# Audio tower on one Trainium2 core: the rows of the first layer normalisation written by GpSimd and not by ScalarE

## The reference, cut to what matters

```
def _layernorm(x, axis=-1, eps=1e-05):
    m = jnp.mean(x, axis=axis, keepdims=True)
    v = jnp.var(x, axis=axis, keepdims=True)
    return (x - m) / jnp.sqrt(v + eps)
...
    h = _L0_tok_ref(x, ...)
    h = h + _L0_attn_ref(_layernorm(h, axis=-1), L0_attn_kernel)
    h = h + _L0_ffn_ref(_layernorm(h, axis=-1), L0_ffn_W1, ...)
```

## Time and profile before

| what | value |
|---|---|
| runs | 116.94, 117.05, 117.34 us; median 117.05 |
| span of the profiled execution | 114.5 us |
| total time of the profiled execution | not printed apart; 117.05 - 114.5 = 2.55 us lie around the span if it is like the median |
| busy shares of the span | PE 83%, DVE 80%, PEld 65%, ACT 59%, POOL 52% |
| mean granted TensorE clock | 0.969 of full speed, full in the middle of the kernel |

### The profile page before, as it was taken

One profiled execution on the slowest core, in us unless ns is written; L12 is line 12 of the kernel. 1 busy time (PEld: TensorE's weight loads), 2 busy tenths in 40 slices (PEclk: granted clock), 3 DMA queues, 4 the chain that ended last, 5 costly groups with the idle time before them and its releaser, 6 DMA issues.

```text
span 114.5 us, 2381 instructions
## 1 busy us (share of the span) xinstructions
PE 94.5 (83%) x618; PEld 74.7 (65%) x618; DVE 91.1 (80%) x335; ACT 67.9 (59%) x207; POOL 59.4 (52%) x122
## 2 busy tenths in 40 slices
PE   6968889899899999999999989997979827994000
PEld 2344367779588888888888979886848625773000
DVE  2789999999999799799797899996899999824000
ACT  3051447946868968968969888947587504550000
POOL 3335795754767767677586565290350996000000
PEclk9999999999999999999999999999999999999755
DMA  3940000000100100100000000000000021333332
GB/s 66 214 172 0 0 0 3 0 11 0 45 0 0 45 0 0 45 0 0 0 3 0 0 0 0 6 0 0 0 0 0 16 77 47 83 100 108 109 108 70
DMA packets 5622, 3.80 MB, mean 33 GB/s; under 512 B 210, under 2 KB 5487, under 8 KB 5615
## 3 DMA queue, kind: packets, MB, share of 16 engines
q1 hardware_dynamic: 5341, 3.40, 10.7%
q10 hardware_dynamic: 274, 0.33, 1.3%
HBM read 1.68 MB, written 2.05 MB: 33 GB/s over the span
## 4 chain that ended last, share of the span: by engine, by line
DVE 40%; PE 25%; POOL 10%; issue 10%; POOLq 3%; ACT 3%; DVEq 1%; ACTq 0%
DVE n L889 8%; PE bank_o L407 6%; DVE scaled L699 4%; PE bank_s L367 4%; DVE neg_max L742 4%; POOL rstd_x L231 4%; POOL rstd L245 3%; DVE h_all L753 3%; DVE bn L706 3%; DVE rinv_keep L749 3%; DVE bn L761 2%; DVE tap L682 2%; DVE mv L767 2%; DVE hb_all L879 2%; PE bank_x L396 2%
## 5 line engine op out<-in xcount | busy, mean ns | idle before, releaser
L574 ACT ACTIVATE a<-bank_s,neg_max 125x250 f32<-125x250 f32 x32 | 13.3, 467 | 8.6 <-DVE neg_max L742 8.4
L386 PE MATMUL bank_o<-v,at 125*125 125x129 f32 x128 | 17.7, 280 | 0.0
L367 PE MATMUL bank_s<-n1t,pt 128*125 128x250 f32 x64 | 16.4, 379 | 0.6 <-ACT pt L563 0.6
L386 PEld LDWEIGHTS bank_o<-v,at 125*125 125x125 f32 x128 | 15.4, 187 | 1.8 <-ACT at L581 0.9
L889 DVE TENSOR_SCALAR n<-h_all,mean,rstd 125x128 f32<-125x128 f32 x32 | 16.0, 564 | 0.0
L552 ACT ACTIVATE n<-h_all,shift,rstd 125x128 f32 (+1 forms) x28 | 12.2, 487 | 0.3 <-POOL shift L250 0.3
L742 DVE TENSOR_REDUCE neg_max<-bank_s 125x2 f32<-125x500 f32 x16 | 10.7, 671 | 2.1 <-PE bank_s L367 1.9
L367 PEld LDWEIGHTS bank_s<-n1t,pt 128*125 128x125 f32 x64 | 10.7, 187 | 1.9 <-ACT pt L563 1.2
L263 POOL TENSOR_TENSOR h_all<-scaled,rows_sb 125x512 f32<-125x512 f32 (+1 forms) x6 | 7.6, 1270 | 8.2 <-DVE scaled L699 8.2
L376 PE MATMUL bank_at<-ident,a 125*125 125x125 f32 x64 | 10.5, 286 | 1.3 <-ACT a L574 1.3
L354 PE MATMUL bank_np<-n1t,qk_w 128*128 128x250 f32 x32 | 9.6, 382 | 1.4 <-ACT n1t L559 1.0
(11 more groups left out here) (111 smaller groups left out, 199.5 us busy)
## 6 DMA issues: line engine op xcount, KB each, us to landing
out_dram<-hb_all SPq DMA_DIRECT2D x7, 250.0 KB
x_head<-x_dram SPq DMA_DIRECT2D x4, 125.0 KB, 5.2
x_slot<-x_dram SPq DMA_DIRECT2D x4, 125.0 KB, 2.1
w_sb<-weights_dram SPq DMA_DIRECT2D x1, 320.5 KB, 5.7
out_dram<-hb_all SPq DMA_DIRECT2D x2, 125.0 KB
rows_sb<-rows_dram ACTq DMA_DIRECT2D x1, 187.5 KB
tok_w<-tok_dram ACTq DMA_DIRECT2D x1, 130.0 KB, 2.7
```

The lines of the kernel that those rows point to most:

```text
L367: last = nc.tensor.matmul(s_ps[par][:, a, :], pt[par][:, a * H:(a + 1) * H], n1t[par][:, :], start=True, stop=True)
L386: last = nc.tensor.matmul(o_ps[:, a, 0:DV], at_sb[par][:, c, a * H:(a + 1) * H], v_sb[par][:, c, :], start=(c == 0), stop=(c == 1))
L574: last = nc.scalar.activation(a_sb[par][:, a, :], s_ps[par][:, a, :], ACT.Exp, bias=neg_max[par][:, a:a + 1])
```

## The change

GpSimd writes n1 of pairs 1 to 7 (14 blocks, 28 instructions), and ScalarE no longer does. The new instruction is a GpSimd `tensor_scalar` on a 125 x 128 tile, h minus mean, times 1/std, with mean and 1/std as one value for each partition. `shift1`, `neg_mean1` and their constant go, with the two instructions of `root_1` that made them. As GpSimd now reads the mean from `mv1`, DVE waits before `aggregate_1` until the second block of the pair before has been written (`n1_ready`). In the DVE loop that wait stands ahead of the second tap. GpSimd's loop over pairs is written out, as the new waits are below one in its first turns.

```diff
@@ root_1
                 pool.tensor_tensor(var1_eps[:, tiles], mv1[:, tiles, 1], eps[:, tiles], ALU.add).then_inc(eps1_ready, m)
-                if after(pair, 1):
-                    pool.tensor_tensor(neg_mean1[:, tiles], mv1[:, tiles, 0], neg_one[:, tiles], ALU.mult)\
-                        .then_inc(negm1_ready, m)
                 pool.wait_ge(eps1_ready, done)
...
-                if after(pair, 1):
-                    pool.wait_ge(negm1_ready, done - 2)
-                    pool.wait_ge(rstd1_ready, done)
-                    pool.tensor_tensor(shift1[:, tiles], neg_mean1[:, tiles], rstd1[:, tiles], ALU.mult)\
-                        .then_inc(shift1_ready, m)
+
+            def normalize_1(pair, par):
+                b = 2 * pair + par
+                pool.wait_ge(rstd1_ready, b + 1)
+                pool.wait_ge(n1t_mm, b - 1)
+                for n in (2 * par, 2 * par + 1):
+                    last = pool.tensor_scalar(n1[par][:, n % 2, :], h_tiles[:, pair, n, :], mv1[:, n, 0:1],
+                                              rstd1[:, n:n + 1], ALU.subtract, ALU.mult)
+                last.then_inc(n1_ready, 1)
@@ gpsimd, head
             first_tap(x_head[:, 3, :])
+            normalize_1(1, 0)
             root_1(1, 1, 1)
@@ gpsimd, turns
-            with pool.Fori(1, NP - 4) as k:
+            for k in range(1, NP - 4):
+                normalize_1(k, 1)
                 root_1(k + 1)
+                normalize_1(k + 1, 0)
                 root_x(k + 2)
...
             for k in range(NP - 4, NP - 2):
+                normalize_1(k, 1)
                 root_1(k + 1)
+                normalize_1(k + 1, 0)
                 root_x(k + 2)
                 add_beta(k + 2)
                 root_2(k - 1)
+            normalize_1(NP - 2, 1)
             root_1(NP - 1)
+            normalize_1(NP - 1, 0)
+            normalize_1(NP - 1, 1)
             root_2(NP - 3)
@@ scalar: normalize_1 and its calls go
             def step(k, xs=True):
-                normalize_1(k, 1)
                 out_p(2 * k, 0)
...
                 out_p(2 * k + 1, 1)
-                normalize_1(k + 1, 0)
                 out_at(2 * k, 0)
@@ vector, before the loop
             dve.wait_ge(bn1_ready, 6)
-            dve.wait_ge(shift1_ready, 2)
+            dve.wait_ge(n1_ready, 4)
             aggregate_1()
@@ vector, loop
                 dve.wait_ge(bn1_ready, 2 * k + 4)
+                dve.wait_ge(n1_ready, 2 * k + 2)
                 second_tap(k + 3, x_slot)
                 aggregate_1()
```

More of the change, by code:

```diff
@@ L100, in audio_tower @@
         eps = sb("eps", [H, 4])
-        neg_one = sb("neg_one", [H, 4])
         one = sb("one", [H, 4])
@@ L124, in audio_tower @@
         var1_eps = sb("var1_eps", [H, 4])
-        neg_mean1 = sb("neg_mean1", [H, 4])
         rstd1 = sb("rstd1", [H, 4])
-        shift1 = sb("shift1", [H, 4])
         n1 = [sb(f"n1_{p}", [H, 2, D]) for p in range(2)]
@@ L172, in audio_tower @@
                              "rstd_x_ready", "x_scaled", "h_ready"))
-        bn1_ready, stats1, eps1_ready, negm1_ready, rstd1_ready, shift1_ready, hb_ready = (
-            sem(n) for n in ("bn1_ready", "stats1", "eps1_ready", "negm1_ready", "rstd1_ready",
-                             "shift1_ready", "hb_ready"))
+        bn1_ready, stats1, eps1_ready, rstd1_ready, hb_ready = (
+            sem(n) for n in ("bn1_ready", "stats1", "eps1_ready", "rstd1_ready", "hb_ready"))
         stats2, eps2_ready, mean2_ready, rstd2_ready = (
@@ L274, in _ @@
             pool.memset(eps[:, :], EPS).then_inc(roots_consts, 1)
-            pool.memset(neg_one[:, :], -1.0).then_inc(roots_consts, 1)
             pool.memset(one[:, :], 1.0).then_inc(roots_consts, 1)
@@ L293, in _ @@
             first_tap(x_head[:, 1, :])
-            pool.wait_ge(roots_consts, 4)
+            pool.wait_ge(roots_consts, 3)
             root_x(0, 0, 1)
@@ L544, in squares @@
                                      accum_out=var_x[:, n:n + 1]).then_inc(xvar_ready, 1)
[L546 to L554, removed]
             def out_n1t(b, par):
@@ L624, in _ @@
             out_v(1, 1)
-            normalize_1(1, 0)
             act.wait_ge(x_mm, 6)
@@ L646, in gelu @@
                 nc.scalar.activation(g_sb[par][:, :], f1_ps[par], ACT.Gelu, bias=b1_col).then_inc(gelu_ready, 1)
-            normalize_1(NP - 1, 1)
             out_p(NB - 2, 0)
```

## The result

The kernel after takes **133.82 us** (median of 4 runs, 132.44 to 134.81) against 117.0 before (4 runs beside them, 116.36 to 117.34). The ratio is 1.1415, with a 95% interval of 1.1349 to 1.1481; it leaves out the run of 134.81, which was in a slower state. The forecast was 123.9 us with a range of 121.3 to 126.7: right on the side, and less than half of the loss (6.9 of 16.8). The profiled execution took 134.32 us, its span 132.6.

A forecast was written before the change was run, and what follows sets the result against it. It took a DVE and GpSimd ring in the loop over pairs as the bound. Terms 0.25 + 0.49 + 4.08 + 1.06 + 0.2 + 0.8 = 6.9 us gave 123.9 us against 117.05, range 121.3 to 126.7.

The forecast's parts named there:

- the price of the new instruction: GpSimd's new tensor_scalar on 128 elements: 0.34 us each, bounds 0.26 and 0.42; a block of two 0.72 until written.
- Part 1, DVE's wait: Second block ahead of root_1, loop turns 2 to 4: DVE waits for n1 before its second tap, +0.97 us a turn.
- Part 2, the rows between the powers: Next pair's first block between GpSimd's two powers: 0.68 us comes in, L250's 0.19 goes, +0.49 a turn.
- The turn: One turn of the loop over pairs grows from 8.41 to 9.77 us; three turns cost 4.08.
- Part 3, the written-out loop: GpSimd's loop written out shortens the gap before add_beta: 0.10 us off a turn, lower bound no gain.
- Part 4, PE's room: ACT's lost instructions gain nothing; PE waits for GpSimd at turn_n1 but has 1.05 us of room in a turn.
- The head: Pair 1's first block on GpSimd meets DVE's L719, which reads two SBUF tensors: 0.25 us, bounds 0 and 0.5.
- The meeting with the four normalisations after turn 6: GpSimd's pair 7 rows meet DVE's four L889, each waiting for one GpSimd instruction: 0.8 us, bounds 0 to 1.2.
- The meetings spread: Rival, chance 0.10: n1's instructions also meet L749 and the multiply-adds every turn, 3.4 us at most, about 126.5 us.
- One of the two delays hides: Rival, chance 0.12: n1 written before DVE arrives, so only the rows between the powers cost in turns 2 to 5; 120.5 us.
- ACT's relief decides: Rival, chance 0.03, faster: only ACT's shorter path counts, 0.33 us in turn 6 and about as much in turn 7; 116.4 us.
- the ring: Loop over pairs: path through DVE and GpSimd returning one turn later, aggregate_1 to GpSimd's L238 to L231, scale_x, next aggregate_1.

The follow-up runs named there:

- run 1: Kernel before with nine groups of four GpSimd tensor_scalar instructions, in different operation pairs and sizes, added behind its last work; no whole-kernel time given.
- run 5: The kernel after, unchanged, measured once more: 132.69 us, ratio 1.136; its table sets its 131.83 us execution against the kernel before.
- run 2: Kernel after with its GpSimd rows as times-plus, neg_mean1 and shift1 made by GpSimd again, all DVE waits kept: 126.35 us, ratio 1.0787.
- run 3: Kernel after with a copy of mv1 for every pair, no DVE wait for n1 before aggregate_1, DVE's loop written out: 127.22 us, ratio 1.0916.
- run 7: The kernel of run 6 with the next pair's first block written behind root_x instead of ahead of it: 117.41 us, ratio 1.0049.
- run 4: Kernel before with only GpSimd's loop over pairs written out: 116.66 us, ratio 0.997.
- run 6: Kernel after with rows as plus-times using a separate negated mean, and no DVE wait for n1 before aggregate_1: 120.93 us, ratio 1.0361.
- run 8: Kernel before, GpSimd's loop written out, GpSimd writing only each pair's second block as times-plus, ScalarE still the first: 117.24 us, ratio 1.0042.
- run 9: Kernel before, GpSimd's loop written out, with the addition for rstd_x and shift1 placed between the two powers: 115.57 us, ratio 0.9874.

## Why the prediction was right about the side and wrong about the size

**The step that failed is "the price of the new instruction".** It took 0.34, with 0.26 and 0.42 as bounds, "since L220 is the same operation". It isn't. L220 multiplies and adds, the new row subtracts and multiplies, and that pair costs 0.78 on 128 elements (run 1; 0.77 in the kernel after, half of 44.43 to 45.97). Twenty such instructions lie on the path by the prediction's own count, so the error is 20 x 0.43 = 8.6 us, and 6.9 + 8.6 = 15.5, against 15.6 between the two spans of run 5's table. That fit is closer than its parts, which miss by up to 0.75 on either side (below). The upper bound failed for the same reason: it was made from two-input rows of another operation. The fixed part of 0.15 was also too small; even the cheap pair costs 0.43 (run 1), just over the upper bound. With the price of times-plus the sum would have been 6.9 + 20 x 0.09 = 8.7 us, or 9.7 with the 0.19 of the shift back in five turns (10.2 with the 0.30 that it takes in run 2's rows); run 2, which is that kernel, lost 9.5 (126.35 against 116.89).

**Part 1, DVE's wait** was right in kind: 0.97 + 0.86 for the dearer pair makes 1.83, and DVE's idle time is 1.96. Run 3, which takes the wait away and writes out DVE's loop, gives 1.16 of 11.50 back.

**Part 2, the rows between the powers** was right: 0.49 + 0.86 makes 1.35, and `scale_x` waits 1.64, which is 1.33 more than the 0.31 of the earlier trace rows. Run 7, which moves them, shows that the price was due to their place.

**The turn**: 9.77 + 2 x 0.86 = 11.49, measured 11.48 and 11.50. Nothing but the price was wrong in it.

**Part 3, the written-out loop**: 0.10 taken, 0.13 in run 4.

**Part 4, PE's room**: right in the loop (the room is 9.77 less 8.8, so 0.97 and not the stated 1.05, which changes nothing). PE has 8.73 of 11.48 busy and waits for n1:

```profile
53.38 0.43 PE L353 MATMUL bank_np<-ident,n 125*128 125x125 f32 x2 [1.83 <-POOL n L246]
...
86.28 0.43 PE L353 MATMUL bank_np<-ident,n 125*128 125x125 f32 x2 [1.36 <-POOL n L246]
```

The second row is block 13, where the prediction had 0.1 of wait, or 1.0 with 0.86 more for the pair. The step to `aggregate_1` of turn 5 is 2.86, where 0.49 + 0.57 + 2 x 0.86 make 2.78. That of turn 6 is 2.71, where 0.49 + 0.4 + 2 x 0.86 make 2.61: the 0.4 was right, and that half of it would hide (0.2) was not.

**The head**: 0.25 was taken for the meeting of POOL's rows with the head's addition to h. That addition takes 0.58 in place of 0.47 (run 5), 0.1. What was missed is turn 1: the dear rows of block 3 hold `aggregate_1` there by 0.75, where the prediction let DVE pass.

**The meeting with the four normalisations after turn 6**, taken at 0.8, didn't happen, though POOL writes four rows at that very time. POOL's row and then DVE's:

```profile
88.32 3.22 POOL L246 TENSOR_SCALAR n<-h_all,mv,rstd 125x128 f32<-125x128 f32 x4
```

```profile
88.56 1.16 DVE L880 TENSOR_SCALAR n<-h_all,mean,rstd 125x128 f32<-125x128 f32 x4
```

They took 1.16, and 1.11 alone. In run 6, with the cheap rows beside them, they took 1.33. The bound of 0 was the better value, and the row that I had used, DVE beside `add_b2`, is another operation again.

**The rivals.** "The meetings spread" is nearest in microseconds and wrong in kind: in the kernel after no meeting costs anything in a turn. It is true of runs 6 to 8 only, and there POOL pays. "One of the two delays hides" came true only where it was made so, in run 7. "ACT's relief decides" fell: in run 8 ACT has 4 us less to do, and neither the time nor turn 6 is shorter.

**What the range left out.** The head at half clock costs 2.5 us in one execution of the kernel after and nothing in another, and run 9's kernel has a late head without the change. How much of it is in the other eight, of which there is no profile, isn't settled. The range of 121.3 to 126.7 missed with or without it.

## What to carry to other kernels

Before work is moved to GpSimd, find a row of the very pair of operations on it, not only of the same instruction: subtract-and-multiply costs 0.78 us on 125 x 128 where add-and-multiply with a negated value costs 0.43, and the result is the same. Read the ring first and place new work in the rests of the receiving engine: moving half of the same 28 instructions from ahead of `root_x` to behind it took the loss from 4.0 us (run 6) to 0.5 (run 7), and a rest shrinks when the other engine's two-tensor instructions run in it. A rest of the writing engine is free only if the reader doesn't need the result sooner: in runs 7 and 8 the turn was still 0.5 longer, because PE waited for rows of the second block, for which it doesn't wait when ScalarE writes them. Where an engine on the ring waits for its own last result, put an independent small instruction there: that was the only change here that gained.

## What the runs showed of the hardware that was not expected

- **The pair of operations sets GpSimd's rate.** 0.86 ns an element for times-plus, 3.5 for minus-times, both with about 0.32 us fixed; on 128 elements the two sets of tensors tried gave the same 0.78 (run 1). One multiplication or one subtraction alone (0.58 on 128 elements) is dearer than a multiplication with an addition (0.43). Why was not tried.
- **The dear form is gentle to DVE.** Beside it, DVE's four `tensor_scalar` took 1.16 (alone 1.11) and its taps 0.48 and 0.45, and the rows were not longer either (run 3). The cheap forms do meet DVE: a row beside the taps takes 0.67 in place of 0.45 (runs 6, 7, 8), and four `tensor_scalar` beside them 1.33. The Trainium skill, "SBUF — State Buffer", section "Who interferes with whom", has a DVE instruction with two inputs in SBUF contend with any GpSimd instruction that reads SBUF. By that rule the cheap rows agree with runs 6 to 8; the dear rows, which read the same tensor, don't agree with run 3. That the meeting depends on how densely GpSimd reads would fit both, but was only argued.
- **The granted clock in the head** can differ between two executions of one program, 0.50 and 1.00 in the same 3.5 us, and the difference is 2.5 us of the whole. In run 9's execution the head is 4.0 us later than before and its matmul rows are as long as at 0.50 (0.79 in place of 0.49), while the clock reads 1.00. What starts it isn't known.
